# The exponentials of a cross-attention, head by head on ScalarE

## The reference

```python
q = x @ Wq.T
k, v = jnp.split(context @ Wkv.T, 2, axis=-1)          # 16 heads of 64
sim = jnp.einsum('bhid,bhjd->bhij', q, k) * SCALE      # 512 rows x 64 keys per head
sim = jnp.where(mask[:, None, None, :], sim, max_neg)
attn = jax.nn.softmax(sim, axis=-1)
out = jnp.einsum('bhij,bhjd->bhid', attn, v)
return out.transpose(0, 2, 1, 3).reshape(B, Nq, -1) @ Wout.T + b_out
```

## Time and profile before

| | us |
|---|---|
| median of 3 runs | 1473.45 |
| lowest and highest | 1471.83, 1474.73 |
| span of the profiled execution | 1471.4 |
| PE busy | 1400.8 (95%) |
| DVE busy | 934.6 (64%) |
| ACT busy | 552.8 (38%) |
| POOL busy | 651.8 (44%) |

### The profile page before, as it was taken

How to read it: one execution, slowest core, us unless ns; L and a number is a source line. 1 busy time by engine, 2 the same in 40 slices (tenths; PEclk the granted TensorE clock), 3 DMA queues, 4 the chain that set the end, 5 groups by cost and what they waited for, 6 DMA issues and landing times. The chain is left out here.

```text
span 1471.4 us, 25544 instructions
## 1 busy us (share of the span) xinstructions
PE 1400.8 (95%) x8404; PEld 1147.4 (78%) x8404; DVE 934.6 (64%) x1891; ACT 552.8 (38%) x1041; POOL 651.8 (44%) x1083
## 2 busy tenths in 40 slices
PE   7978999999999999999999999999849999999998
PEld 5756777777787777777778787777648899998897
DVE  5535878878778687787877878788635332233323
ACT  2023434354344444435434453444333322233312
POOL 0124556556465564555646556465442211222111
PEclk9998999999999999999999999999979999999999
DMA  8621001111011110111101111030013011110100
GB/s 262 156 62 29 30 25 41 40 34 40 23 48 33 33 43 22 43 39 33 41 23 47 34 37 37 29 115 23 22 26 115 1 58 58 57 57 11 46 0 30
DMA packets 116953, 70.02 MB, mean 48 GB/s; under 512 B 73569, under 2 KB 114274, under 8 KB 116834
## 3 DMA queue, kind: packets, MB, share of 16 engines
q1 hardware_dynamic: 113714, 66.75, 15.1%
q10 hardware_dynamic: 3120, 1.71, 0.4%
HBM read 42.22 MB, written 26.21 MB: 47 GB/s over the span
## 5 line engine op out<-in xcount | busy, mean ns | idle before, releaser
L1367 POOL TENSOR_TENSOR w_lo<-w_raw,w_hi 128x2048 fp32r<-128x2048 f32 x16 | 73.8, 4609 | 241.1 <-ACT w_hi L1318 192.3
L131 PE MATMUL ob<-b_hi,pT_hi 128*128 128x256 f32 x512 | 159.7, 312 | 6.5 <-DVE pT_lo L731 6.3
L793 POOL TENSOR_TENSOR prob<-prob,rz 128x512 f32<-128x512 f32 x128 | 131.0, 1045 | 76.5 <-DVE rz L690 76.5
L1340 ACT ACTIVATE hT_hi<-up 128x512 fp32r<-128x512 f32 x128 | 76.1, 597 | 236.3 <-PE up L133 236.3
L738 POOL TENSOR_SCALAR ve<-mv 128x1 f32<-128x1 f32 x256 | 56.5, 221 | 224.7 <-DVE mv L648 217.1
L742 POOL TENSOR_TENSOR rstd<-ve,epsc 128x1 f32<-128x1 f32 x256 | 144.9, 566 | 23.9 <-POOL ve L738 5.1
L1529 DVE SCALAR_TENSOR_TENSOR hT_lo<-up,hT_hi 128x512 fp32r<-128x512 f32 x128 | 88.2, 691 | 96.8 <-ACT hT_hi L1340 96.8
L131 PE MATMUL dn<-w_hi,hT_hi 128*128 128x256 f32 x512 | 145.0, 283 | 0.8 <-DVE acc L1538 0.8
L132 PE MATMUL dn<-w_lo,hT_hi 128*128 128x256 f32 x512 | 144.9, 283 | 0.0
L133 PE MATMUL dn<-w_hi,hT_lo 128*128 128x256 f32 x512 | 144.9, 283 | 0.0
L132 PE MATMUL ob<-b_lo,pT_hi 128*128 128x256 f32 x512 | 144.8, 283 | 0.0
(11 more groups left out here) (215 smaller groups left out, 3740.4 us busy)
## 6 DMA issues: line engine op xcount, KB each, us to landing
xraw<-in_x SPq DMA_DIRECT2D x16, 512.0 KB, 4.1
kv_scratch<-stage SPq DMA_DIRECT2D x32, 256.0 KB, 2.6
x_scratch<-x SPq DMA_DIRECT2D x64, 128.0 KB, 1.8
out_x<-o_sb SPq DMA_DIRECT2D x64, 128.0 KB, 1.7
w_raw<-in_L_ffn_experts_inter SPq DMA_DIRECT2D x8, 1024.0 KB, 5.0
w_raw<-in_L_ffn_experts_out SPq DMA_DIRECT2D x8, 1024.0 KB, 7.5
kraw<-kv_scratch SPq DMA_DIRECT2D x32, 128.0 KB, 2.7
vraw<-kv_scratch SPq DMA_DIRECT2D x32, 128.0 KB, 2.9
```

The lines of the kernel that those rows point to most:

```text
L131: pe.matmul(out, lh, rh, start=first, stop=False)
L793: pool.tensor_tensor(part, part, rz[:, q, h * 8:h * 8 + 8].unsqueeze(2).broadcast_to([P, 8, NKV]), ALU.mult).then_inc(s["p_ready"], 1)
L1340: act.activation(hT_hi[:, h, i, :], up[i % 4][:, :], ACT.Relu).then_inc(s["up_hi"], 1)
L1367: pool.tensor_tensor(lo[:, u, :, :], raw[:, :, :], f32(hi[:, u, :, :]), ALU.subtract).then_inc(s["w_lo_made"], 1)
```

## The change

The shift on DVE and the sum over `prob` go away. The maximum is written negated. ACT reads the scores in PSUM itself, one head at a time: 8 exponentials of 64 columns a half, with the head's negated maximum as the bias and the sum accumulated into the head's column of `zsum`. The scores' bank is given back by ACT (`sim_taken`) after the eighth. The reciprocal waits for that semaphore, and the exponentials of half 0 wait until the reciprocal of the tile before was made, since `zsum` has one buffer.

```diff
     def act_exp(act, n, q, h):
-        need(act, "sim_taken", 2 * n + h + 1)
-        act.activation(prob[:, q, h * HK:(h + 1) * HK], prob[:, q, h * HK:(h + 1) * HK],
-                       ACT.Exp).then_inc(s["exp_made"], 1)
+
+        need(act, "max_made", 2 * n + h + 1)
+        if h == 0:
+            need(act, "rz_made", n)
+        for g in range(HEADS // 2):
+            head = h * (HEADS // 2) + g
+            last = act.activation(prob[:, q, head * NKV:(head + 1) * NKV], sim[h][:, g * NKV:(g + 1) * NKV], ACT.Exp,
+                                  bias=mx[:, head:head + 1], scale=1.0, accum_out=zsum[:, head:head + 1])
+        last.then_inc(s["sim_taken"], 1)
...
             dve_max(dve, n, 0)
         prep("a")
         if has_sim:
-            dve_shift(dve, n, q, 0)
             dve_max(dve, n, 1)
-            dve_shift(dve, n, q, 1)
...
-            need(dve, "exp_made", 2 * n + 2)
-            dve.tensor_reduce(zsum[:, :], prob[:, q, :].rearrange("p (g j) -> p g j", j=NKV),
-                              AX.X, ALU.add).then_inc(s["sum_made"], 1)
-            dve.wait_ge(s["sum_made"], n + 1)
+            need(dve, "sim_taken", 2 * n + 2)
             need(dve, "p_ready", 2 * n - 2)
             dve.reciprocal(rz[:, q, :], zsum[:, :]).then_inc(s["rz_made"], 1)
...
-        dve.tensor_reduce(mx[:, h * 8:h * 8 + 8], by_head(sim[h][:, :]), AX.X, ALU.max).then_inc(s["max_made"], 1)
-
-    def dve_shift(dve, n, q, h):
-
-        dve.wait_ge(s["max_made"], 2 * n + h + 1)
-        dve.tensor_tensor(by_head(prob[:, q, h * HK:(h + 1) * HK]), by_head(sim[h][:, :]),
-                          mx[:, h * 8:h * 8 + 8].unsqueeze(2).broadcast_to([P, 8, NKV]),
-                          ALU.subtract).then_inc(s["sim_taken"], 1)
+        dve.tensor_reduce(mx[:, h * 8:h * 8 + 8], by_head(sim[h][:, :]), AX.X, ALU.max, negate=True
+                          ).then_inc(s["max_made"], 1)
```

More of the change, by code:

```diff
@@ L189, in setup_and_attention @@
         "z_made", "z_taken", "x1_ready", "x1_biased",
-        "sim_made", "max_made", "sim_taken", "exp_made", "sum_made", "rz_made", "p_ready",
+        "sim_made", "max_made", "sim_taken", "rz_made", "p_ready",
         "pt_made", "pt_hi_made", "pt_taken", "o_made", "o_taken",
```

## The result

The changed kernel takes 1533.55 us in the median (1531.03 to 1535.34), the kernel before 1473.51: a ratio of 1.040, 95% interval 1.038 to 1.042. It is 60 us slower. The forecast was 1533.

A forecast was written before the change was run, and what follows sets the result against it. PE was taken to bound the attention loop. Lateness of 3.57 us a batch over 14 batches (50) plus 9.5 in the last two gave 59.5; with the 1471.4 span and 2.05 to the median, 1533; 8-in-10 range 1487 to 1605.

The forecast's parts named there:

- PE sets the pace: Attention loop: PE is the bound, about 59.7 us a batch; DVE and ACT cost nothing if copies arrive in time.
- The price of a head: ACT's queue: one head's exponential with accumulated sum holds it 0.305 us, two halves 4.88 us.
- The free sum: Rival, ACT: accumulated sum costs nothing, 0.20 us a head, only slot 3 late by 1.17, 1489; chance 0.16 with one-third price.
- the sum in series without overlap: Rival, ACT: the sum is a full serial instruction, 0.42 us a head, 10.1 us a batch, 1637; chance 0.14.
- Slots: Loop: PE late by 0, 0.47, 0.25 and 2.85 us in slots 0 to 3, 3.57 us a batch.
- the way from slot 2 to slot 3: Late `s_bc` in slot 2 delays GpSimd's product, and so slot 3's first normalisation on ACT, by 1.0 us.
- my formula: Slot 3, ROW waiting for `sbd`: lateness is the two halves' queue time minus 2.03 us, giving 2.85.
- a stall before `pt`: Sign of being wrong: PE's stall sits before `pt`, through the single bank of transposes.
- The rest: Last two batches: ACT's chain is the longer, estimated at 1.2 us a tile, 9.5 us.
- the rival of the falling clock: Rival, loop: stalls halve PE's clock once a batch, some 1.5 us each, 21 us more, 1555; chance 0.14.
- Faster: Rival, last batches: DVE without its sum makes `pT_lo` 1 sooner, gaining 7 us, 1466; chance 0.03.

The follow-up runs named there:

- the last version: Kernel before, with one maximum per row and half as exponential bias, and the sum behind `pT_lo` 1 in the last two batches only: 1470.65 us.

## Why the prediction came out

**PE sets the pace: right.** Taking DVE's shifts away (row maximum) or giving its sum back (without the accumulator against without the pointer) leaves each slot of the loop as it is. It holds for work taken away; the sum moved behind `pT_lo` 1 cost slot 3 0.5 us. The row quoted for it, is one trip with two batches and not two trips; 59.7 us a batch follows all the same.

**The price of a head: right, with a term off.** Exponential to read 0.196 us against 0.20 worked out from rows; the read 0.093 against 0.106. The free sum, and the sum in series without overlap, are both excluded by the starts. Two halves hold 4.62 us, not 4.88. One pointer is 0.092 (0.196 against 0.104), as the 88 ns of the prediction. The Trainium skill, "ScalarE: Activation LUTs", What ACT_TABLE_LOAD costs, gives about 93 ns for a pointer, and the runs agree; on the cost of the accumulator, as much again, the page gives no figure.

**Slots.** Late by 0, 0.4, 0.1 and 2.8 us for slots 0 to 3, against 0, 0.47, 0.25 and 2.85. In 14 batches 47 us against 50. In slot 3, 0.2 of the 0.26 us that two halves were cheaper were made up: the exponentials start at 6.92 and not at 6.84, and the record of `sbd` behind the chain is 0.53 long and not 0.40.

**One step was wrong: the way from slot 2 to slot 3.** The size was right (the first normalisation of slot 3 is 1.1 us later, from 4.4 to 5.5 after the slot's start), the mechanism was not: it isn't GpSimd's product, it is `pT_lo` 1 and DVE's queue behind it (`s_bc` earlier by itself gave nothing, the two normalisations later in slot 2 gave 0.8). This has a consequence. I had taken the 1.0 us as fixed, whatever a head costs. It isn't: with 0.196 a head, where `pT_lo` 1 of slot 2 is done at 9.3 and not at 10.7, the first normalisation of slot 3 starts at 4.4 in every batch, as before the change. That is why the kernels with 0.196 a head are late by 0.3 in slot 3, where my formula and the rival of the free sum said 1.2 to 1.3; a free sum would have cost some 5 us in the loop and not 16.

The stall in slot 3 is also spread: 0.67 before `x1T`, 0.3 before `pT` 1 and 1.43 before ROW, where I had put 2 to 3 us before ROW and had named a stall before `pt` as a sign of being wrong; it is there, as the smallest of the three. Each earlier wait makes the later ones shorter; the last place still sets the sum.

**The rest: too small.** 14.4 us against the estimate of 9.5. Part of it is the clock, shown by the stretch from batch 14 to the experts, the changed kernel first and then the one before (busy us of the engines, then the granted clock):

```profile
1026.00:1153.00 127.00, 94.17 (x527) 75.53 (x526) 57.06 (x133) 70.64 (x323) 53.60 (x112) 0.89 0.14 40
```

```profile
978.20:1091.00 112.80, 87.51 (x527) 69.62 (x526) 76.32 (x158) 43.91 (x84) 53.82 (x112) 0.94 0.14 40
```

PE's clock is granted 0.89 against 0.94: the longer idling there falls together with more time at 1.2 GHz. The same 527 records of PE add up to 6.7 us more, and 7.5 us are more idling (32.8 against 25.3). By these two figures, an estimate since the ends of matmuls are modelled, the lateness itself was not above the 9.5, and what the term left out was the slower clock. No experiment separates the two. In the loop, the rival of the falling clock was wrong for the changed kernel: a batch that neither holds nor follows a loop branch is 63.1 us long (15.1 + 15.9 + 12.3 + 19.8), the sum of its short slots. Only at the loop's branches was there more of it, 3 stretches at 1.2 GHz in 5 trips against 1 before. It came true with the second pointer, where PE idles 2.0 us before T0 and 2.2 before ROW: 15 falls, 25 us, where I had priced 14 falls and 21.

**Faster: wrong in the changed kernel, right as a mechanism.** The sum does stand ahead of `pT_lo` in the last batches: taken out of the way there alone, with the shifts gone, it gives what the last version gained, 3 us by the medians and 4.8 in the profiled execution, where the prediction had 7. That 47 and 14 were off by 3 and 5 in opposite directions, and the head by 5%, is part of why 1533 was met so closely.

## What to carry to other kernels

When one engine sets the pace, work put on another isn't priced by its busy share but by the last value it hands over in each stage: add up its queue from the event that starts it to the copy that the pacing engine waits for, and compare with when that engine needs it. Below the threshold the work is free, above it each microsecond counts fully, and moving what nobody waits for behind the copies can give nearly as much as removing work (41 of 60 us here, where taking out the sums gave 48). The same chain can run through a second engine into the next stage, as it did here over DVE. A short exponential with a pointer and an accumulated sum holds the queue nearly three times as long as one without: 0.104 us for 64 columns (from its start to that of its read), 0.092 more for the pointer, 0.093 for the read.

## What the runs showed of the hardware

An accumulated sum on ACT is an instruction of its own. Its record is 257 ns long on average, but it holds the queue for 0.093 us. Records of a chain of short exponentials grow from 0.31 to 0.42 us while the starts stay 0.29 apart, and the copies behind the chain have records up to 0.12 longer (0.595 us before, 0.71 behind the chain). Why, no run shows. So a record's length is no measure of how long an instruction holds the queue; the distance between starts is. Stalls of 1.4 to 1.5 us before ROW, once a batch, did not bring PE's clock down; with stalls of 2.2 to 2.3 us at the same place it fell in 9 of 14 batches, each time at a price of 1.7 us. The length of this stall doesn't decide: it was 2.2 us in the 9, 2.3 in four of the other five and 2.2 in the fifth. The 9 and the fifth are the 10 batches of the loop, the four are the unrolled ones. I don't know what decides.
